# One picked source tile a window in layers 1 to 3 of a graph network kernel, in place of two

## The reference, cut to what matters

```
h  = relu(layernorm(x));  ea = edge_attr @ eencW + eencb;  xl = h @ encW + encb
for l in 0..3:                       # genconv; layers 1 to 3 on a normed input, added to xl
    m     = relu(h[src] + ea) + 1e-7
    alpha = softmax of m*t[l] over the edges of one destination, per feature
    h1    = segment_sum(m*alpha, dst) + h
    out   = relu(ln(h1 @ W1 + b1)) @ W2 + b2
x = x + relu(ln(xl)) @ linW + linb;  h = relu(layernorm(x))
x = x + segment_sum(h[dst] * edge_weight, src)
```

## Time and profile before

| | |
|---|---|
| median of the runs | 11827.7 us |
| the profiled execution, its own time | 11828.1 us |
| its span | 11826.3 us |
| mean granted TensorE clock | 0.694 |
| PE / PEld busy | 5802.2 us (49%) / 4077.1 us (34%) |
| DVE busy | 6551.7 us (55%) |
| ACT busy | 3327.1 us (28%) |
| POOL busy | 6522.0 us (55%) |
| DMA | 1354.58 MB, mean 115 GB/s |

### The profile page before, as it was taken

The page is one execution under the profiler, slowest core; times in us unless marked ns, Lnnn a source line. Parts: engine busy times, 40 slices in busy tenths (PEclk is TensorE's granted clock), DMA queues, the critical chain, the costliest instruction groups (busy, mean ns, idle before and its releaser), DMA issues. The chain is left out here.

```text
span 11826.3 us, 107787 instructions
## 1 busy us (share of the span) xinstructions
PE 5802.2 (49%) x31762; PEld 4077.1 (34%) x31762; DVE 6551.7 (55%) x8055; ACT 3327.1 (28%) x4948; POOL 6522.0 (55%) x6157
## 2 busy tenths in 40 slices
PE   2333333343444444444444444444444447888887
PEld 2222222232333333333333333333333334444443
DVE  5666666664444444544444445444444457998897
ACT  1333333342333333333333333333223232111110
POOL 5455455535444444454544444544444446888887
PEclk6666666666666666666666666666666668999998
DMA  5344344333333333333333333333333334555555
GB/s 155 125 137 138 123 140 132 130 109 103 118 117 117 117 117 117 102 97 116 119 118 118 117 118 106 95 117 118 117 117 117 117 112 94 99 97 99 96 94 86
DMA packets 840467, 1354.58 MB, mean 115 GB/s; under 512 B 499934, under 2 KB 556476, under 8 KB 838730
## 3 DMA queue, kind: packets, MB, share of 16 engines
q1 hardware_dynamic: 523832, 1135.94, 27.5%
q0 software_dynamic: 312640, 214.30, 12.9%
q10 hardware_dynamic: 3916, 3.40, 0.1%
HBM read 806.66 MB, written 546.46 MB: 114 GB/s over the span
## 5 line engine op out<-in xcount | busy, mean ns | idle before, releaser
L826 POOL DMA_INDIRECT xg<-h_tab,idx x4656 | 4461.7, 958 | 4370.0 <-DVE idx L1159 2909.3
L917 PE MATMUL turn<-hb,hot 125*128 125x192 bf16 x12480 | 1872.5, 295 | 3018.0 <-issue 2977.7
L917 PEld LDWEIGHTS turn<-hb,hot 125*128 125x128 fp8e4 x12480 | 1310.6, 114 | 3571.7 <-issue 3536.0
L1159 DVE COPY idx<-idx_full 128x24 int32 x208 | 36.6, 176 | 3526.7 <-ACT zl L1035 3526.7
L933 PE MATMUL turn<-ident,sums 128*128 128x128 f32 x5184 | 1073.7, 375 | 1533.8 <-ACT st_all L1050 1140.4
L1524 POOL DMA_INDIRECT acc<-vm,tgt x1026 | 1602.9, 1562 | 341.2 <-issue 288.1
L933 PEld LDWEIGHTS turn<-ident,sums 128*128 128x128 f32 x5184 | 878.0, 222 | 1676.3 <-ACT st_all L1050 1243.6
L1066 ACT ACTIVATE hx<-turn 128x384 bf16<-128x384 f32 x156 | 76.4, 490 | 3600.9 <-PE turn L917 3553.1
L1050 ACT ACTIVATE st_all<-turn 128x512 f32<-128x512 f32 (+1 forms) x1344 | 752.3, 577 | 698.7 <-PE turn L933 321.0
L1166 DVE TENSOR_TENSOR_SCAN rx<-rp,carry,zl 128x1536 f32<-128x1536 bf16 (+1 forms) x224 | 739.9, 3303 | 360.1 <-ACT zl L1035 343.1
L1597 PE MATMUL zl<-spreadz,lo_hot 128*128 128x512 f32 x1620 | 765.5, 609 | 95.2 <-DVE spreadz L1773 95.2
(11 more groups left out here) (277 smaller groups left out, 7413.2 us busy)
## 6 DMA issues: line engine op xcount, KB each, us to landing
sums<-st_all SPq DMA_DIRECT2D x208, 1536.0 KB
hot<-hot_tab SPq DMA_DIRECT2D x312, 625.0 KB
ea<-feat SPq DMA_DIRECT2D x158, 768.0 KB
srcB<-src_flat SPq DMA_DIRECT2D x108, 768.0 KB
rp<-run_pen SPq DMA_DIRECT2D x210, 384.2 KB
xg<-h_tab,idx POOLq DMA_INDIRECT x4656
hot_tab<-hot SPq DMA_DIRECT2D x104, 625.0 KB
run_head<-zeros SPq DMA_DIRECT2D x216, 192.0 KB
```

Of the source, the lines that this page charges most:

```text
L826: g_.indirect_dma_start(xg[b][:, k, h, :], None, h_tab[:, :], bass.IndirectOffsetOnAxis(ap=idx[b][:, h, k:k + 1] if small is None else idx ...
L917: ins = pe.matmul(picked[:, :, n % 2, :], hot[n][0:PN, t_, :], hb[0:PN, t_, :, :], start=t_ == 0, stop=t_ == NT - 1, skip_group_check=True)
```

## The change

It sets one picked tile in layers 1 to 3, made in layer 0 with one comparison a window, and leaves out the last layer's store of the node rows, with the waits adjusted.

```diff
-HOT = [0, 2, 2, 2]
-MADE_IN = [0, 0]
+HOT = [0, 1, 1, 1]
+MADE_IN = [0]
@@ layer(), on SP
-                        for k in range(NCH):
+                        for k in range(NCH if l + 1 < L else 0):
                             sp.wait_ge(h_ok, NCH * l + k + 1)
                             store_nodes(k)
@@ after the layers, on SP
-                    sp.wait_ge(tab_out, 16 * NCH * L + 16)
+                    sp.wait_ge(tab_out, 16 * NCH * (L - 1) + 16)
+                    sp.wait_ge(h_ok, NCH * L)
```

## The result

Median of the changed kernel 11709.45 us (11655.94 to 11713.41), of the kernel before, run beside it, 11825.72 us: ratio 0.9898, 95% interval 0.9870 to 0.9925. That is a gain of 116 us, where 508 us were forecast. The profiled execution is the fastest of its runs: 11655.94 us, span 11654.0, 172 us under the one before.

The account below looks back on a forecast made before the run. A chain of waits was taken as the bound, with PE and ACT starved of instructions during gathers. Savings of 480 + 12 + 10 + 2 = 504 us from 11828.1 gave about 11,320 us, range 10,950 to 11,880.

Parts of the forecast that it names:

- Select halves: Layers 1 to 3: 40 select matmuls instead of 80 finish about 7.6 us after zl, leaving the starved stretch altogether.
- hx comes early: Layers 1 to 3: the copy hx comes 23.7 us sooner and half as wide, and keep can follow it.
- What is late next: Rest of forward on PE: with about six matmuls of instruction stock, it ends 28 to 37 us after the first gather.
- One gather more: Full windows: one more gather costs 1.26 us; gathers last 28.6 us, and starvation ends 32.6 us after the first.
- The new period: Layers 1 to 3, zl to zl: 39.0 us against 42.2, bounds 36.0 and 41.0; saves 480 us over 150 periods.
- rival B: Small gain: hx and keep stay in the chain behind the starved stretch; 41.0 us a period, 11,620 us total; chance 0.20.
- Last period: Last period of each layer's loop, 25.0 us before: the select's late matmuls go, about 4 us each, 12 in all.
- Layer starts: Start of each layer: two windows' gathers 2.5 us longer, first select 40 matmuls shorter; 0, plus or minus 5 each.
- Layer 0: Layer 0's windows: one comparison (5.49 us) and one store less; between -135 and +45 us, taken as -10.
- rival C: Slower: gathers of successive windows close up, so work falls behind the following gathers; 43.3 us a period, 11,970 us; chance 0.19.
- Node rows: End of the last layer: without the node-row store, SP no longer waits for its landing; saves 2 us.
- D: Same time: select's starvation was never on zl's path; 11,828 us plus or minus 24; chance 0.05.

Follow-up runs that it names:

- the run with both tables: Changed kernel, but layer 0 makes and stores both tables as before: 11500.02 us, 0.9817 of the kernel before, on the slower kind of chip.
- the hold run: Changed kernel, but in layers 1 to 3 POOL starts a full window's gathers only once hx is copied: 10699.1 us, 0.9128 of before (slower chips); 8887.23 us, 1.0127 (faster).

## Why the prediction was right or wrong

- *Select halves:* right. It leaves the starved stretch, in one piece, 9.5 us after zl's start (its idle fell to 65 us; under 400 was forecast).
- *hx comes early:* wrong, and this is the step that failed. I took a matmul that has run for a matmul that is known to have run. ACT could not start hx 23.7 us sooner, because the increment it waits for comes only 3.9 us behind the gathers, 26 us after the last matmul. The trace of before already held the proof, in the semaphore event of tile n = 0 and in SP's load at 5558.97 that waits for it; the lines of the earlier trace rows don't show it. I had explained all idle time by instructions that lack.
- *What is late next:* I asked whether PE had stock for forward. It had (eight of the eleven transposes ran from 5238.09, the rest needs hx); it did not matter.
- *One gather more:* right, 28.7 us against 27.4.
- *The new period:* from the first gather 28.7, to hx 3.9, from hx to u 1.6, u 3.0, zl 1.6, and 1.35 to the next gather: 40.2 in the window shown, 40.5 in the mean, and not 39.0. The upper bound of the step, 41.0, has the chain that ran, with hx and keep on it: keep follows hx, and u follows keep without idle. It was 0.8 us too long, with 2.0 for hx and keep where 1.6 passed and 0.4 of hand-over that is not in the rows. So the bound was right and my middle value was not: rival B's figures (41.0, 11,620) hold with another reason. Its reason, the loop's end, is out: that end stands in every second window, and 147 of the 150 hx copies in the loops wait 25.1 to 26.5 us, with and without it.
- *Last period:* right in kind, -18 against -12. *Layer starts:* 0, as forecast, and by luck: the sum of two parts of 90 us each that I had not seen. One is the first period, 67 us long, in which hx waits 56 to 58 us behind the gathers of two windows.
- *Layer 0:* the mechanism was right and its size mis-set. I gave the closing of the pause 8 us in a third of the windows against 5.5 us gained, and took -10; a joined pair takes 96.4 us against 2 x 44.6 = 89.2, and most pairs join: +99 us. That rests on the run with both tables, which undoes it; why a joined pair costs what it does is argued and not tested. The cause of rival C was true in layer 0; in layers 1 to 3, where I had placed it, the pause stayed 11.5 us.
- *Node rows:* -2, right.
- The Trainium skill ("Runtime: NRT & Kernel Launch", Instruction fetch mechanics) holds straight fetching to be hidden. Chip B agrees: 40 matmuls in 3.51 us beside gathers. Chip A would not, with singles 1.4 to 3.5 us apart in the hold run, if what PE lacks there are instructions; the rows say only "issue", and no run here shows what they stand for.
- *Two bounds in the recorded working* don't follow from its own terms: 38 to 40.2 us a period gives 11,174 to 11,504 us (it has 11,130 to 11,480), and halfway from D to C is 11,899 us (it has 11,880). Neither decides anything here.

Steady windows gained 228 us less than forecast and layer 0 cost 109 us more: together 337, which is the miss of the profiled execution (504 against 172, with 5 of small terms).

## What to carry to other kernels

An instruction that has run is not yet one that others know of. Where engines stand still together, read when the semaphore's event was recorded, not only when the work ended, and see who else waits for it: two waiters that start together point at a late semaphore. Where such a stall hangs on a background stream, place the stream, by one wait on what must come first, before cutting the work; here that was worth 8% where the cut was worth 1%. And compare on more than one chip: the change gained 1% on one kind, and on the other, measured with the hold on both sides, it cost 1.2%.

## What the hardware showed that I had not expected

- On chip A, PE's increments for work done in a burst of indirect DMAs come late. In layers 1 to 3 the select's comes 3.9 us after the burst (2.6 with half of the gathers), 26 us after the matmul in the steady windows and up to 58 us in the first period of a layer. Within the long bursts of layer 0 they come within the burst, one in some 10.5 us and 15 to 25 us late. ACT's (preload to PE's transposes, 0.14 us) and DVE's (0.03 us to ACT's exponentials) come at once in the same burst. On chip B, PE's come in 0.02 us.
- The onset is not immediate: in the changed kernel PE's increments came at once up to 2.7 us after the first gather (the next was due at 6.5 us and was late), with the hold up to 7.7 us. What sets it was not tried.
- The same program takes 11,708 to 11,826 us on some chips and 8774 to 8777 us on others. With plain loads in the full windows of layers 1 to 3 these windows are equal. Why the chips differ stays open.
